# Storing the last half tile of the output from two queues, 64 partitions from each, instead of from one queue

## What is computed

```python
def _L0_xattn_ref(teacher_logits, teacher_features, Wq, bq, Wk, bk):
    query = jnp.einsum('bnc,dc->bnd', teacher_features, Wq) + bq
    key = jnp.einsum('bnc,dc->bnd', teacher_features, Wk) + bk
    attention = jax.nn.softmax(jnp.einsum('bnd,bmd->bnm', query, key), axis=-1)
    return jnp.einsum('bln,bmn->blm', teacher_logits, attention)
...
    xn = (x - mean) * jax.lax.rsqrt(var + EPS) * ln_weight + ln_bias
    out = jnp.einsum('bsk,ok->bso', xn, jnp.sign(weight)) * jnp.max(jnp.abs(weight)) * gamma + beta
...
    x = x + jnp.tanh(g_xattn[0]) * _L0_xattn_ref(_layernorm(x), ctx_1024, Wq, bq, Wk, bk)
    x = x + jnp.tanh(g_ffn[0]) * _L0_ffn_ref(_layernorm(x), weight, gamma, beta, ln_weight, ln_bias)
```

## Time and profile before

| | |
|---|---|
| median of three runs | 123.03 us (122.89 to 123.53) |
| the profiled execution's own time | 122.83 us |
| its span, first to last instruction | 121.0 us |
| granted TensorE clock over the span | 0.999 |
| busy: TensorE matmuls, VectorE, ScalarE, GpSimd | 116.7, 95.3, 85.8, 97.4 us |
| DMA: bytes read and written in HBM | 12.59 MB, 4.19 MB |

### The profile page before, as it was taken

One profiled execution on the slowest core, in us unless ns is written; L12 is line 12 of the kernel. 1 busy time (PEld: TensorE's weight loads), 2 busy tenths in 40 slices (PEclk: granted clock), 3 DMA queues, 4 the chain that ended last, 5 costly groups with the idle time before them and its releaser, 6 DMA issues.

```text
span 121.0 us, 1903 instructions
## 1 busy us (share of the span) xinstructions
PE 116.7 (96%) x570; PEld 95.2 (79%) x570; DVE 95.3 (79%) x190; ACT 85.8 (71%) x183; POOL 97.4 (80%) x111
## 2 busy tenths in 40 slices
PE   7999999999999999999999999999999999999980
PEld 6578888788888888888889788878888888888870
DVE  0389979897996994698948982998859939989991
ACT  3456899999998979178998794569997962246200
POOL 2559998939169989999976999984748999999970
PEclk9999999999999999999999999999999999999999
DMA  3999599861651400038741302548000022220045
GB/s 109 347 341 333 183 396 353 275 219 56 175 206 52 156 17 5 5 154 272 267 171 62 116 0 87 173 173 259 1 0 5 5 79 94 87 87 0 0 159 188
DMA packets 10109, 17.15 MB, mean 142 GB/s; under 512 B 1522, under 2 KB 2036, under 8 KB 10100
## 3 DMA queue, kind: packets, MB, share of 16 engines
q1 hardware_dynamic: 9808, 16.78, 40.1%
q10 hardware_dynamic: 292, 0.26, 0.7%
HBM read 12.59 MB, written 4.19 MB: 139 GB/s over the span
## 4 chain that ended last, share of the span: by engine, by line
PE 95%; DVE 2%; ACT 0%; issue 0%
PE ps_y L449 37%; PE ps_ffn L462 23%; PE ps_score L384 7%; PE ps_turn L416 6%; PE ps_score L416 3%; PE ps_score L539 3%; PE ps_y L416 3%; PE ps_turn L331 2%; PE ps_y L407 2%; PE ps_ffn L407 2%; PE ps_ffn L346 2%; PE ps_score L393 1%; PE ps_turn L384 1%; PE ps_y L531 1%; PE ps_ffn L478 1%; DVE ctx_sb L862 1%
## 5 line engine op out<-in xcount | busy, mean ns | idle before, releaser
L955 POOL TENSOR_TENSOR xt_lo<-xt_raw,xt_hi 128x512 fp32r<-128x512 f32 x16 | 22.0, 1377 | 5.5 <-ACT xt_hi L590 3.2
L449 PE MATMUL ps_y<-pt_hi,xt_hi 128*128 128x512 f32 x64 | 18.0, 402 | 0.0
L449 PE MATMUL ps_y<-pt_hi,xt_lo 128*128 128x512 f32 x64 | 17.5, 395 | 0.0
L449 PE MATMUL ps_y<-pt_lo,xt_hi 128*128 128x512 f32 x64 | 17.5, 395 | 0.0
L462 PE MATMUL ps_ffn<-w_sign,zt_hi 128*128 128x512 f32 x60 | 17.2, 409 | 0.0
L578 ACT ACTIVATE prob<-ps_score,neg_max 128x512 f32<-128x512 f32 x14 | 9.5, 682 | 10.1 <-DVE neg_max L726 10.1
L462 PE MATMUL ps_ffn<-w_sign,zt_lo 128*128 128x512 f32 x60 | 16.5, 396 | 0.0
L449 PEld LDWEIGHTS ps_y<-pt_lo,xt_hi 128*128 128x128 f32 x64 | 12.0, 188 | 2.9
L449 PEld LDWEIGHTS ps_y<-pt_hi,xt_lo 128*128 128x128 f32 x64 | 12.0, 188 | 2.9
L793 DVE SCALAR_TENSOR_TENSOR ffn<-ps_ffn,rstd,gain 128x512 f32<-128x512 f32 x14 | 10.4, 744 | 4.6 <-PE ps_ffn L462 3.1
L449 PEld LDWEIGHTS ps_y<-pt_hi,xt_hi 128*128 128x128 f32 x64 | 11.7, 189 | 2.4
(11 more groups left out here) (196 smaller groups left out, 274.6 us busy)
## 6 DMA issues: line engine op xcount, KB each, us to landing
xt_raw<-in_x_t_dram SPq DMA_DIRECT2D x16, 256.0 KB, 2.9
ctx_sb<-in_ctx_t_dram SPq DMA_DIRECT2D x8, 256.0 KB, 4.6
x_sb<-in_x_dram SPq DMA_DIRECT2D x8, 256.0 KB, 4.3
ctx_sb<-in_x_dram SPq DMA_DIRECT2D x8, 256.0 KB, 5.8
out_dram<-x SPq DMA_DIRECT2D x8, 256.0 KB, 2.0
out_dram<-ctx_sb SPq DMA_DIRECT2D x7, 256.0 KB, 2.0
w_raw<-in_weight_t_dram SPq DMA_DIRECT2D x4, 256.0 KB, 6.7
ln_w<-in_ln_weight_dram SPq DMA_DIRECT2D x1, 256.0 KB, 5.5
```

Of the source, the lines that this page charges most:

```text
L449: mm = pe.matmul(ps_y[t % 2][:, :], lhs[:, t, k, :], rhs[:, k, :], start=(k == 0 and i == 0), stop=(k == KN - 1 and i == 2))
L955: nc.gpsimd.tensor_tensor(xt_lo[:, t, :, :], xt_raw[:, t, :, :], xt_hi[:, t, :, :].bitcast(f32), ALU.subtract).then_inc(xt_lo_done, 1)
```

## The change

The store of the last half of tile 3 is cut by partitions. ScalarE stores partitions 0 to 63 (64 KB), and SyncE, after its store of the first half, waits for the same count of `last_out_done` and stores partitions 64 to 127 (64 KB). SyncE's final wait goes from 32 to 48, since three DMAs now count `last_stored` up. Nothing else is touched.

```diff
@@ SyncE
             sp.dma_start(out[B - 1, t * P:(t + 1) * P, halves[0]], x1_buf[(B - 1) % 2][:, t, halves[0]])\
               .then_inc(last_stored, 16)
-            sp.wait_ge(last_stored, 32)
+            sp.wait_ge(last_out_done, 3)
+            sp.dma_start(out[B - 1, t * P + P // 2:(t + 1) * P, halves[1]],
+                         x1_buf[(B - 1) % 2][P // 2:, t, halves[1]]).then_inc(last_stored, 16)
+            sp.wait_ge(last_stored, 48)
@@ ScalarE
             act.wait_ge(last_out_done, 3)
-            act.dma_start(out[B - 1, (T - 1) * P:, halves[1]], x1_buf[(B - 1) % 2][:, T - 1, halves[1]])\
-               .then_inc(last_stored, 16)
+            act.dma_start(out[B - 1, (T - 1) * P:(T - 1) * P + P // 2, halves[1]],
+                          x1_buf[(B - 1) % 2][:P // 2, T - 1, halves[1]]).then_inc(last_stored, 16)
```

## The result

The changed kernel takes 123.80 us as a median of 20 runs (123.01 to 124.34), the kernel before 123.04 in 20 runs beside them (122.33 to 123.88). The ratio is 1.0049, with a 95% interval of 1.0029 to 1.0069, so the change costs 0.6 us (0.4 to 0.85). A second comparison, of 12 runs with 35, gave 1.0028 (1.0001 to 1.0055). The prediction said 123.2 us and a range of 122.7 to 123.6: the side was right, the size too small, and the median lies outside the range.

The account below looks back on a forecast made before the run. The prediction took the DMA engines' rate over unchanged bytes to bound the kernel's end, not the issue. Its terms, 0 + 0 + 0.2 = +0.2 us, gave 123.2 us as a median, with a range of 122.7 to 123.6.

Parts of the forecast that it names:

- Issue on ScalarE: In the tail, ScalarE's issue of half the rows still begins at 118.56, at worst takes the same 0.38 us: 0.
- New issue on SyncE: In the tail, SyncE's added issue begins at 118.69, first packet 119.5 to 119.9, needed by 119.92: 0.
- Data, +0.2 us: The last 128 KB, read from 64 partitions per piece, move at the exchange's 209 GB/s, less an overlap allowance: +0.2 us.
- The 0.3 us behind it stay.: From the last store's landing to the end of the span, the 0.3 us were to stay unchanged.
- Rival A: Last store: 64 partitions as quick as 128, or the pieces overlap; no change, 123.0 us as a median; chance 0.27.
- B: Last store: the two queues' pieces go side by side, saving 0.19 us, 122.8 as a median; chance 0.05.
- C: Last store: the two issues hold each other up, SyncE's packets come after 119.92; +0.58 us, 123.6 median; chance 0.07.
- D: Last store: a 64-partition store uses few of the 16 engines; with half of them 0.38 us more, 123.4; chance 0.03.
- What would show it: Signs in the tail's profile: DMA engines busy without a gap, last stretch at 200 to 270 GB/s, last landing some 120.9.

Follow-up runs that it names:

- even/odd kernel: The changed kernel, but ScalarE stores the even partitions of the last half tile and SyncE the odd ones; ratio 1.0016 to the kernel before.
- tile 2 in halves: The kernel before, with GpSimd adding the last batch's tile 2 in two column halves, stored by ScalarE (first, once done) and SyncE; ratio 0.9981.

## Why the prediction was wrong

- **What bounds the kernel.** Right that only the tail can change, and that the engines are busy without a pause in it. "The end is set by the DMA engines' rate over bytes that don't change, not by the issue" was half right. With 128 KB moved forward the landing stayed, so the time at which packets are ready was a bound of about the same size.
- **Issue on ScalarE, "at worst it takes the same 0.38 us ... 0".** Wrong: 0.57, for half the rows, and the first packet comes 1.22 us after the issue, where a lone piece of 128 partitions needs 0.88. I took fewer rows to be cheaper and used the 0.59 us of the exchange only for SyncE's. The slack of 0.3 us that ScalarE's store had behind SyncE's bytes is used up by it, and the engines stand idle for 0.06 us before its packets come.
- **New issue on SyncE, "in time by either row: 0".** Wrong too. I allowed SyncE's piece until 119.92, which is 1.39 us after the last addition, with a first packet 1.2 us after its issue, 0.03 us before it would be missed. It came at 1.54 to 1.57, since the preparing of ScalarE's piece stands ahead of it. In the changed kernel that cost only some 0.03 us, because ScalarE's slow packets kept the engines busy so long. At the full rate late packets cost more: the even/odd kernel has 0.15 us of idle engines and still lands 0.18 us late.
- **Data, +0.2 us.** The mechanism is right: 207 GB/s from 64 neighbouring partitions in a store, and it measured +0.15 us of packet time for each engine. The landing moved by 0.24, close to the forecast's 0.2, and part of that closeness is luck: the term was 0.05 too large, and the two issues set to nothing cost 0.09.
- **"The 0.3 us behind it stay."** This is the step that failed outright: +0.24 us, as much as the whole landing. A wait and a store were said to cost SyncE nothing, because nobody queued behind them; but they made its program one instruction longer.
- **The sum:** 0.15 (data) + 0.09 (the two issues) + 0.24 (the close) = 0.48 us in the tail, where the forecast has 0.2 + 0 + 0. The landing's part alone would give some 123.3 us, inside the range.
- **Rival A** (nothing) and **B** (faster) fall by the landing, at +0.24 us. B's ground, that there is no time to spare, holds. **C** was right that SyncE's packets come later than 119.92 (they come 0.15 to 0.18 us later), but its price was too large, and most of the idle time lies ahead of ScalarE's packets; its reason, the issues holding each other up, is wrong (0.53 and 0.60 us from one engine alone), and what is serial is the preparing behind them. **D** falls: both pieces finish with 16 completions each, one at each engine.
- **What would show it.** The rate (184 to 256 GB/s against "200 to 270") was as forecast. The last landing less the last addition is 2.33 us, against 2.3 to be read from the forecast. Another mark of the forecast failed: the engines were to be busy without a gap until the last byte, and their share was 0.80 to 0.84. No mark looked behind the last landing, where half of the cost is.

The Trainium skill's rule (DMA: Bandwidth & Descriptors, Rules for kernel authors), to use one transfer of 128 partitions and not two to disjoint halves, is borne out. Its reason, shared engines, gives no loss by itself; here the losses are the rate, the preparing, and SyncE's close.

No version beat the kernel before: the best, tile 2 in halves, is at 0.9981 (0.9954 to 1.0008).

## What to carry to other kernels

Cutting a last store in two halves by partitions shortens nothing: each piece costs as much or more to prepare, the pieces are prepared in turn even from two queues, and 64 neighbouring partitions are read at half rate. Before a store is sped up, look at what is there when its packets could come first: bytes ahead of it, or the preparing of the DMAs ahead of it. And to judge a change of a few tenths of a microsecond at the end, compare a stretch of the trace that doesn't scatter (here from the last addition on), since whole times scatter by more than 1 us. Take that stretch to the very end of the program: here one instruction more on the engine that closes it cost as much as all that happened to the data. And when two causes overlap, add up busy and idle time within one trace, since taking one cause away shows only what the other leaves of it.

## What the runs showed of the hardware that I had not expected

- A store from 64 partitions took 0.50 to 0.60 us to issue and 1.16 to 1.26 us to its first packet (longer right behind another engine's); one from 128 partitions, with twice the rows, 0.33 to 0.48 and, from engines at rest, 0.8 to 0.9. Neighbouring or every second partition made no difference to this.
- Two such DMAs issued at the same moment from ScalarE and SyncE had first packets some 0.3 us apart, both with neighbouring and with even and odd partitions.
- Packets of 1 KB took 47 to 50 ns on average from 128 or every second partition, and 62 to 72 ns in pieces of 64 neighbouring ones.
- SyncE paused for 0.3 to 0.4 us ahead of its 80th recorded instruction in ten traces of kernels long enough to have one. In an eleventh a wait for the landing hides the place.
